# A graph layer on one core: the one-hot gather goes from 8 wide slots a block to 13 slots of two destinations

## The reference, cut to what matters

```python
h = jnp.maximum(_layernorm(x, axis=-1), 0.0)
xs = h[src]
for r in range(4):
    w_r = jnp.where(edge_type == r, edge_weight, 0.0)
    total_msg = total_msg + (xs @ W_rel[r] + b_rel[r]) * w_r[:, None]
agg = segment_sum(total_msg, dst, 625)
agg = agg / jnp.maximum(segment_sum(edge_weight, dst, 625), 1.0)[:, None]
x1 = _layer_norm(h + h @ W_self + b_self + agg, ln1_g, ln1_b)
out = x + _layer_norm(x1 + gelu(x1 @ W_ffn1 + b_ffn1) @ W_ffn2 + b_ffn2, ln2_g, ln2_b)
```

## Time and profile before

| | us |
|---|---|
| median of 3 runs (270.31 to 273.2) | 271.7 |
| the profiled execution, whole | 273.55 |
| its span | 271.4 |

### The profile page before, as it was taken

How to read it: one execution, slowest core, us unless ns; L and a number is a source line. 1 busy time by engine, 2 the same in 40 slices (tenths; PEclk the granted TensorE clock), 3 DMA queues, 4 the chain that set the end, 5 groups by cost and what they waited for, 6 DMA issues and landing times.

```text
span 271.4 us, 3721 instructions
## 1 busy us (share of the span) xinstructions
PE 257.7 (95%) x1443; PEld 212.9 (78%) x1443; DVE 207.1 (76%) x351; ACT 64.1 (24%) x86; POOL 24.6 (9%) x50
## 2 busy tenths in 40 slices
PE   7969999999999999999999998999999999999990
PEld 7857877787887887788887787778888999978770
DVE  2567599698759996899899989995572878955544
ACT  2447111505334014010110220104240663300000
POOL 3193000000000000000010001001020000003211
PEclk9959999999999999999999999999999999999996
DMA  7951232314000510000000000000171075001121
GB/s 188 294 136 65 78 77 80 80 32 127 2 0 1 170 69 1 2 4 0 0 4 3 1 2 4 2 0 3 26 236 51 0 241 146 2 0 38 38 66 47
DMA packets 9453, 15.74 MB, mean 58 GB/s; under 512 B 2413, under 2 KB 2633, under 8 KB 9432
## 3 DMA queue, kind: packets, MB, share of 16 engines
q1 hardware_dynamic: 9168, 15.13, 19.1%
q10 hardware_dynamic: 264, 0.33, 0.6%
HBM read 14.03 MB, written 1.28 MB: 56 GB/s over the span
## 4 chain that ended last, share of the span: by engine, by line
PE 72%; DVE 17%; issue 3%; DMA 3%; DVEq 2%; SPq 1%; ACT 1%; POOL 0%; POOLq 0%; ACTq 0%
PE ps L997 70%; DVE wp L706 4%; DVE keq L701 3%; DMA x<-in_x 3%; DVE eqp L695 3%; DVEq L583 2%; DVE AT_lo L749 1%; SPq L337 1%; DVE wring L580 1%; DVE slot L683 1%; DVE x L761 1%; PE ps L1145 1%; PE ps L1074 1%; PE ps L1004 1%; ACT AT_hi L489 1%
## 5 line engine op out<-in xcount | busy, mean ns | idle before, releaser
L997 PE MATMUL ps<-wring,hT 128*125 128x512 f32 x300 | 75.6, 407 | 2.9 <-DVE hT L601 2.3
L997 PEld LDWEIGHTS ps<-wring,hT 128*125 128x125 f32 x300 | 55.9, 191 | 17.7 <-issue 2.5
L997 PEld LDWEIGHTS ps<-keq,wp 125*128 125x128 f16 x400 | 35.7, 100 | 11.1 <-issue 7.9
L997 PE MATMUL ps<-keq,wp 125*128 125x240 f16 (+5 forms) x400 | 41.9, 261 | 1.7 <-DVE wp L706 1.6
L997 PE MATMUL ps<-T_hi,AT_hi 125*125 125x512 f32 x100 | 40.3, 403 | 0.0
L997 PE MATMUL ps<-T_lo,AT_hi 125*125 125x512 f32 x100 | 39.5, 395 | 0.0
L701 DVE TENSOR_TENSOR keq<-iota_win,slot 125x2240 f16<-125x2240 f16 x25 | 32.9, 1318 | 0.0
L706 DVE TENSOR_TENSOR wp<-eqp,slot 125x1024 f16<-125x1024 f16 x50 | 32.1, 683 | 0.0
L489 ACT CAST AT_hi<-ps 128x1500 fp32r<-128x1500 f32 (+1 forms) x10 | 12.4, 1237 | 64.2 <-PE ps L997 64.2
L997 PE MATMUL ps<-T_hi,AT_lo 125*125 125x512 f32 x100 | 25.9, 404 | 0.0
L997 PEld LDWEIGHTS ps<-T_lo,AT_hi 125*125 125x125 f32 x100 | 18.6, 186 | 4.2
(11 more groups left out here) (130 smaller groups left out, 305.3 us busy)
## 6 DMA issues: line engine op xcount, KB each, us to landing
stage<-in_L_gnn_W_rel SPq DMA_DIRECT2D x8, 512.0 KB, 3.6
stage<-in_L_gnn_W_ffn SPq DMA_DIRECT2D x8, 512.0 KB, 4.0
x<-in_x SPq DMA_DIRECT2D x5, 224.0 KB
x_again<-in_x SPq DMA_DIRECT2D x5, 224.0 KB
out<-ybuf SPq DMA_DIRECT2D x5, 224.0 KB
stage<-in_L_gnn_W_self SPq DMA_DIRECT2D x2, 512.0 KB, 7.6
g_bc<-in_L_gnn_ln_g SPq DMA_DIRECT2D x2, 256.0 KB, 8.4
b_bc<-in_L_gnn_ln_b SPq DMA_DIRECT2D x2, 256.0 KB, 8.3
```

The lines of the kernel that those rows point to most:

```text
L997: return nc.tensor.matmul(o, l, r, start=start, stop=stop, skip_group_check=True)
```

## The change

Each block gets 13 **slots** of two destinations (the last of one), 325 in all. For each slot 128 consecutive edges are chosen on the chip. The edge data lie in 125 partitions of 165 edges, each followed by the first 95 of the next partition (`EW = 260`). VectorE compares each slot's first destination with the destination at every 33rd edge (`ahead`, 6 operations), and the difference of neighbouring comparisons is a 0/1 matrix `chosen`, with a single 1 for each slot over 125 partitions x 5 offsets. TensorE multiplies the edge fields in 16 bits (source and type in one number, destination, weight high, weight low) by it: 25 products in place of the 15 transposes. VectorE makes the keys from the results, doubled in pairs (`pairs`). A block is then read from `pairs` at a fixed place: no register loads and no `slot` copy. The weights are multiplied into the key side, which is now the small one (`kw`, 2 x 13 x 40), `eqp` (13 x 128) is the stationary side, and TensorE makes 26 products of 40 columns a block (the last two of 20). Also changed: the count compares the number of edges found with the number there are, the edge loads are 8 transfers in place of 4 (four on SyncE's queue, ahead of two weight loads, four on ScalarE's), the bias loads 12 in place of 15, and the order of relation and source tile in A is swapped.

```diff
@@ VectorE, start @@
             low_part(0)
-            link(v.tensor_scalar(TF[:, 1, :], raw[:, 0, :], 0.5 - EK / 2, 1.0 / EK, ALU.add, ALU.mult))
+            dve.wait_ge(iotas, 1)
+            for j in range(EG + 1):
+                i = v.tensor_scalar(ahead[0:TN, j, :], slot_d[0:TN, :], edge_d[:, j:j + 1], None, ALU.is_gt)
+            link(i)
             hT_low(0)
...
             hT_low(1)
-            link(v.tensor_scalar(TF[:, 1, :], TF[:, 1, :], TO_INTEGER, -TO_INTEGER, ALU.add, ALU.add))
...
+            v.tensor_tensor(chosen[0:TN, :, :], ahead[0:TN, 0:EG, :], ahead[0:TN, 1:EG + 1, :],
+                            ALU.subtract).then_inc(choice, 1)
...
             low_part(1)
-            dve.wait_ge(first_in, 1)
-            r = firsts(0)
...
-            dve.wait_ge(eT, 1)
-            for f0, f1 in ((0, 3), (3, 5)):
-                i = v.tensor_copy(
-                    fields[0:EK, f0:f1, 0:ET].rearrange("e f (p g) -> e f g p", g=EG),
-                    FIELDS[f0 // 3].rearrange("e (f g p) -> e f g p", f=f1 - f0, g=EG))
-                i.then_inc(turned, 1)
+            dve.wait_ge(picked, 1)
+            link(v.tensor_scalar(Qt[0:EK, :], F_ps, ROW0 - (TN - 1) / 2, 1.0 / TN, ALU.add, ALU.mult))
+            link(v.tensor_scalar(Qt[0:EK, :], Qt[0:EK, :], TO_INTEGER, -TO_INTEGER, ALU.add, ALU.add))
+            link(v.tensor_tensor(drt[0:EK, :], D_ps, slot_d[0:EK, :], ALU.subtract))
+            v.scalar_tensor_tensor(out=pairs[0:EK, 0, :, :], in0=by_two(Qt[0:EK, :]), scalar=float(-TN),
+                                   in1=by_two(F_ps), op0=ALU.mult, op1=ALU.add)
...
@@ VectorE, a block @@
-                v.tensor_tensor(slot[0:EK, :, :, :],
...
-                v.tensor_tensor(by_pairs(keq[0:EK, b % RING, :, :, :].rearrange("e s q d -> e s (q d)")),
-                                by_pairs(iota_win[0:EK, :, :, :].rearrange("e s q d -> e s (q d)")),
-                                spread(1, TR * WD // 2), ALU.is_equal)
...
-                    i = v.tensor_tensor(by_pairs(wp[0:EK, b % RING, part, :, :]), by_pairs(eqp[0:EK, :, :]),
-                                        spread(2 + part, P // 2), ALU.mult)
+                v.tensor_tensor(keq[0:EK, :, :, :], iota_q[0:EK, :, :].unsqueeze(1).broadcast_to([EK, SL, TR, SW]),
+                                pairs[0:EK, 1, at, :].unsqueeze(2).broadcast_to([EK, SL, TR, SW]),
+                                ALU.is_equal).then_inc(key_in, 1)
+                dve.wait_ge(key_in, b + 1)
                 for part in range(2):
+                    i = v.tensor_tensor(kw[0:EK, z, part, :, :, :], keq[0:EK, :, :, :],
+                                        pairs[0:EK, 2 + part, at, :].unsqueeze(2).broadcast_to([EK, SL, TR, SW]),
+                                        ALU.mult)
                 i.then_inc(blk_in, 1)
@@ TensorE, a block @@
-                        last = mm(o[:, :, lo:hi], wp[0:EK, b % RING, part, j, :], keys, j == 0 and part == 0,
-                                  j == SL - 1 and part == 1)
+                        last = mm(o[:, :, lo:hi], eqp[0:EK, b % RING, j, :], kw[0:EK, b % RING, part, j, :, 0:hi - lo],
+                                  j == 0 and part == 0, j == SL - 1 and part == 1)
@@ TensorE, in place of the transposes @@
+            def pick(o, f, s0, s1):
+                for g in range(EG):
+                    i = mm(o, DF[0:TN, f, ES * g:ES * g + EK], chosen[0:TN, g, s0:s1], g == 0, g == EG - 1)
+                return i
...
+            pick(F_ps, 0, 0, NS)
+            pick(D_ps, 1, 0, NS)
+            pe.wait_ge(w_low_in, 1)
+            pick(WH_ps, 2, 0, NS)
+            pick(WL_ps[0], 3, 0, LH)
+            pick(WL_ps[1], 3, LH, NS).then_inc(picked, 1)
```

More of the change, by code:

```diff
@@ L35, in gnn_layer @@
     ROWS_IN = 16 * len(SPANS)
-    EK = TN
-    ET = E // EK
-    EG = 3
-    EP = ET // EG
+    EC = E // TN
+    ES = 33
+    EG = EC // ES
+    EK = P
+    EW = ES * (EG - 1) + EK
+    assert EC * TN == E and EG * ES == EC
     BW = 25
@@ L46, in gnn_layer @@
     NB = NT * HB
-    SL = 8
+    SW = 2
+    SL = -(-BW // SW)
+    NS = NB * SL
+    SLOT_COLS = [(SW * j, min(BW, SW * (j + 1))) for j in range(SL)]
     GROUPS = [[0, 1, 2], [3, 4]]
@@ L92, in gnn_layer @@
     b1_bc = sb("b1_bc", [P, D], F32, 166)
-    wp = sb("wp", [P, RING, 2, SL, P], F16, 168)
-    keq = sb("keq", [P, RING, SL, TR, WD], F16, 176)
-    iota_win = sb("iota_win", [P, SL, TR, WD], F16, 184.75)
-    eqp = sb("eqp", [P, SL, P], F16, 189.25)
-    fields = sb("fields", [P, 5, ET + SL], F32, 191.25)
-    slot = sb("slot", [P, 4, SL, 2], F16, 194.75)
+    eqp = sb("eqp", [P, RING, SL, P], F16, 168)
+    kw = sb("kw", [P, RING, 2, SL, TR, SW], F16, 174.5)
+    keq = sb("keq", [P, SL, TR, SW], F16, 178.75)
+    pairs = sb("pairs", [P, NF, NS, 2], F16, 180)
+    gfields = sb("gfields", [P, 5, EC], F32, 185.25)
+    iota_gen = sb("iota_gen", [P, TR, BW], F16, 188.5)
+    iota_q = sb("iota_q", [P, TR, SW], F16, 189.5)
+    gkeys = sb("gkeys", [P, TR, BW], F16, 189.75)
+    ghot = sb("ghot", [P, P], F16, 190.75)
+    gw = sb("gw", [P, 2, P], F16, 191)
     brel = sb("brel", [P, D], F32R, 200)
@@ L358, in _ @@
                 load_x(c)
+            sp.wait_ge(tails, 1)
+            for f, vec in ((0, src), (2, etype)):
+                flat = vec.rearrange("(p e) -> p e", p=TN)
+                sp.dma_start(raw[0:TN, f, 0:EC], flat).then_inc(src_in, 16)
+                sp.dma_start(raw[0:TN - 1, f, EC:EW], flat[1:TN, 0:EW - EC]).then_inc(src_in, 16)
             load(1)
@@ L367, in _ @@
             for row in SUM_ROWS:
-                for t in range(NT):
-                    sp.dma_start(brel_raw[row + t * R:row + (t + 1) * R, :], b_rel).then_inc(brel_in, 16)
+                for r in range(R):
+                    sp.dma_start(brel_raw[row + r * NT:row + (r + 1) * NT, :],
+                                 b_rel[r:r + 1, :].broadcast_to([NT, D])).then_inc(brel_in, 16)
             for u in range(STAGES, U_REL):
@@ new lines, in _ @@
+            link(v.tensor_scalar(drt[0:EK, :], drt[0:EK, :], -1.0, float(SW), ALU.max, ALU.min))
+            v.scalar_tensor_tensor(out=pairs[0:EK, 1, :, :], in0=by_two(Qt[0:EK, :]), scalar=float(K_STEP),
+                                   in1=by_two(drt[0:EK, :]), op0=ALU.mult, op1=ALU.add)
+            for half, s0, s1 in ((0, 0, LH), (1, LH, NS)):
+                i = v.tensor_copy(pairs[0:EK, 3, s0:s1, :],
+                                  WL_ps[half].unsqueeze(2).broadcast_to([EK, s1 - s0, 2]))
@@ new lines, in _, with build @@
+            i.then_inc(keyed, 1)
+            def build(b):
+                at, z = slice(SL * b, SL * (b + 1)), b % RING
+                if b >= RING:
+                    block_used(dve, b - RING)
+                v.tensor_tensor(eqp[0:EK, z, :, 0:OW].rearrange("e s (n z) -> e s n z", z=2),
+                                iota_p[0:EK, 0:OW].rearrange("e (n z) -> e n z", z=2).unsqueeze(1)
+                                .broadcast_to([EK, SL, OW // 2, 2]),
+                                pairs[0:EK, 0, at, :].unsqueeze(2).broadcast_to([EK, SL, OW // 2, 2]),
+                                ALU.is_equal).then_inc(eq_in, 1)
@@ L803, in _ @@
             self_add(1)
-            dve.wait_ge(iotas, 1)
-            dve.wait_ge(turned, 2)
-            build(0, r[0])
+            dve.wait_ge(iotas, 2)
+            dve.wait_ge(w_pairs, 1)
+            dve.wait_ge(keyed, 1)
+            build(0)
             for c in range(2, NT):
@@ L833, in _ @@
+            build(1)
             dve.wait_ge(vcnt, 1)
-            v.tensor_copy(f_i32[:, NB:NB + 1], COUNT).then_inc(regs_in, 1)
+            link(v.tensor_scalar(vdiff, COUNT[:, 0:1], -1.0, float(E), ALU.mult, ALU.add))
+            v.scalar_tensor_tensor(out=f_i32[:, 0:1], in0=vdiff, scalar=0.0, in1=COUNT[:, 1:2], op0=ALU.max,
+                                   op1=ALU.add).then_inc(regs_in, 1)
             low_part(4)
@@ L851, in block @@
                     if not general_path:
-                        build(b, first[0][i])
+                        build(b)
                     elif i in LAST:
```

332 lines of the change are left out of this document (136 added, 196 removed).

## The result

| | before | with the change |
|---|---|---|
| median of 4 runs, us | 272.45 (270.31 to 273.57) | 256.48 (255.95 to 256.68) |
| profiled execution, us | 273.55 | 256.68 |
| its span, us | 271.4 | 254.9 |

The ratio is 0.9419 with a 95% interval of 0.9354 to 0.9484: 16 us faster, where 259 us and a range of 253 to 268 were forecast. The spans differ by 16.5 us, where the sum had 12.9. The profiled execution of the kernel before is a slow one of its kernel (mean granted clock 0.979, where 31 executions of it beside the experiments had 0.984 to 0.997 and spans of 267.4 to 270.6 us), so a part of the 16.5 us may be that execution's; the medians differ by 16.0 us here and by 15.2 us in experiment 11.

What follows compares the result with a forecast made beforehand. It took TensorE's queue to bound the middle, VectorE close behind, and the start as a third bound. +4.0 - 14.8 - 2.1 = -12.9 us from 273.55 gives 260.65; less 1.85 for that execution, 258.8, in round 259 us, range 253 to 268.

Steps and rivals of the forecast that it cites:

- Blocks on TensorE: 25 blocks in TensorE's queue: 26 pairs of 35 ns each, 0.91 us in place of 1.50, -14.8 us (-20 to -10.3).
- Blocks on VectorE: VectorE's block build: 2.1 us in place of 3.3, 30 us over all blocks, worth only the end of TensorE's waits.
- the waits for `wp`: Three places where TensorE waited for VectorE's weighted tile: they go, -2.1 us.
- The start: Everything before block 0: six operations ahead of `hT_low(0)`, choosing products, keys and waits for self additions, +4.0 us (+2 to +8).
- the low end of the sum: Whole kernel, best case: -20 + 2.5 - 2.1 = -19.6 us, giving 252 us.
- Block 2 behind the branch: Sign against TensorE being fed too slowly: block 2, directly behind a branch, lasts 1.68 us like block 3.
- TensorE cannot be fed so fast: Every block: 26 small pairs in a row meet a floor near 75 ns, 1.95 us a block, 284.9 us; chance 0.13.
- the estimate from the 62 ns a product: TensorE's blocks: at the skill's 62 ns a product a block is 1.61 us and the time 276 us.
- the clock falls at the new wait: TensorE's waits between 38 and 44 us: 7 us at half clock would cost 3.5, 262.3 us; chance 0.15.
- pairs at 50 to 55 ns: TensorE's blocks: 1.35 us each, so they only pay for the start, 270 us; chance 0.06.
- the general path taken: If a slot's edges did not fit its 128, 25 x 165 steps would run, far over 500 us; chance 0.01.

Runs made afterwards that it cites:

- experiment 11: The changed kernel itself again, in six executions, against the kernel before on the same chip: 256.02 us to 271.26, ratio 0.9450.
- Experiments 1 and 2: Changed kernel with every block product issued twice (first), 274.65 us; changed kernel without the 13 products of the weights' low halves a block (second), 246.78 us.
- experiment 3: Changed kernel with each 40-column product split into two of 20 columns, 50 pairs a block: 271.48 us, ratio 1.0024 to the kernel before.
- experiments 4 and 5: Changed kernel with one unread VectorE comparison more a block, 262.78 us; changed kernel without the branch, weights multiplied into the source side again, 262.98 us.
- the six profiles above: Profiles of kernels with the change's own order up to block 0; in them block 0 began between 46.91 and 48.58 us.
- Experiment 7: Changed kernel with `low_part(2)` and two self additions moved ahead of VectorE's key operations: 253.51 us, ratio 0.9359 to the kernel before.
- Experiments 6 and 8: Changed kernel without branch and general path, 254.94 us; Experiment 7 with the fast path directly behind the branch and the general path kept, 252.20 us.
- experiment 9: Changed kernel with the edge weights' maximum behind the row statistics and TensorE's product on it behind eight transposes: 255.02 us, ratio 0.9369.

## Why the prediction was right, and where it was off

The sign, the places and the range were right, and two errors partly cancelled: the blocks gave 4.6 us more than forecast and the branch took back 1.4. By the steps of the prediction:

- **Blocks on TensorE: the mis-sized term.** The forecast was 35 ns a pair and -14.8 us; it is 28 ns and -19.4, close to the low end (27 ns, -20). The step that failed is the choice of the value: I took it near the 33 ns between two weight loads at the start of a block. But those were the first two after a wait, not loads in a running row, and the recorded ends, 0.10 and 0.13 us, give 30 ns to the nearest 10, not 33. The other estimate in the same paragraph, half of an 80-column pair of 40 ns or a little above, is what 40 columns cost. Experiments 1 and 2 give 28 ns from the whole time, for more pairs and for fewer; experiment 3 shows 25 ns at half the columns.
- **Blocks on VectorE.** `eqp` was forecast near 1.0 us and the others near 0.43; recorded are 1004, 422 and 426 ns. From 104 to 185 us TensorE waits for nothing, so the waits for `wp` are gone, -2.1 us. What the text did not say, and experiments 4 and 5 showed, is that without VectorE's saving 6 to 8 of the 16 us would not have come.
- **The start.** Forecast +4.0, measured +3.9, and that it is so close is luck: by the six profiles above it would be +3.1 to +4.7. Six small operations took 1.37 us (forecast 1.2). The first product came 1.9 us later (forecast 0.8): `hT_low(0)` followed the start of these operations by 1.40 us in place of 0.37, and they themselves began 0.87 later, behind a `wmax` that waited for its transfer. At the choosing 0.9 us were left (31.09 for 30.17; forecast 0.4). The choosing took 33.88 - 31.09 = 2.79 us (2.97), the keys 4.1 us (4.5), and the wait for the self addition was 1.94 us recorded, 2.1 between starts (2.3), with another 0.4 among the 30 products behind it (0.6). Experiment 7 gave 2.2 of these 3.9 us back. The columns of the choosing were priced at 0.42 to 0.46 ns; the 80-column steps of 35 and 40 ns give 0.44 and 0.50, so the 0.42 has no row behind it, though the 2.79 us measured are 0.43 a column. And the low end of the sum has +2.5 for the start where the text has +2, which moves it by 0.5 us.
- **The branch: a missed term, +1.4 us.** Block 2 behind the branch lasted as long as block 3, and I used this as a sign that TensorE is not starved of instructions there. That was the wrong place to look: the stops stand ahead of the block and eight products behind it, and block 2 of the changed kernel lasts as long as its others too. I did not ask what ten more pairs a block do there. Experiments 6 and 8 take the stops away, by removing the branch or by turning it.
- **Rival "TensorE cannot be fed so fast".** It fell: 26 and 52 pairs run at 28 ns. With it fell the estimate from the 62 ns a product that the Trainium skill (TensorE: Matmul & The Clock Gate, section "Wait — 56ns, not 53.3ns?") gives for decoding in software. In a weak form it exists, 25 ns at 20 columns, and as the stops behind the branch.
- **Rival "the clock falls at the new wait".** It did not happen in the two profiles of the changed kernel, nor in those of experiments 1 to 6, where TensorE waited 1.93 or 1.94 us at this place and the granted clock stayed at 1.00 from 38 to 48 us; in the change the 30 products behind the wait took 7.63 us. It did happen in that of experiment 9 after a wait of the same length: the granted clock was 0.50 (1.2 GHz) from 39.6 to 43.0 us and the same 30 products took 8.78 us. One of nine such waits: the chance of 0.15 was fair, and the price was 1.15 us rather than 3.5, since the stretch was 3.4 us and the 0.4 us of waiting among these products went with it. What decides between the two is open. Not forecast was a lower mean granted clock of the changed kernel: 0.973 to 0.980 in its ten executions, 0.984 to 0.997 in the 31 of the kernel before beside the experiments. Where in those executions the difference stands is not on record.
- **The other two rivals** (pairs at 50 to 55 ns; the general path taken) show in no row: pairs are 28 ns apart, and the profile has the fast path's 650 products of a block's form, 25 blocks of 26.

## What to carry to other kernels

Price a row of small products with a fresh 16-bit weight load each by the spacing of starts inside a running row, here 28 ns at 40 columns and 25 at 20, not by recorded durations or by the first two behind a wait: between 40 and 20 columns, splitting work into more pairs costs each pair nearly in full. When the bounding engine gets faster, the saving on the engine beside it is a condition and has to be costed as such, by what TensorE would wait without it. Put work that needs nothing new ahead of an engine's wait (2.2 us here), and the likely path directly behind a branch (0.6 to 1.5 us here). And before two profiles are compared instruction by instruction, look at where their granted clock was at half.

## What the runs showed of the hardware that was not expected

- A load of 128 columns in 16 bits and a product of 20 columns together take 25.4 ns (50 in a row), of 40 columns 27.5 ns (52 in a row), while the load is recorded as 97 ns and the product as 190.
- Behind a branch to a path that lies far off, TensorE stopped 0.41 us ahead of a block of small pairs and 1.05 us eight products behind it. The same path placed first had no such stop, with the branch still there.
- Two executions of the same kernel had a granted clock of 0.50 for 6.8 and for 10.2 us at the start, so that first products at 17.77 and 16.88 us led to block 0 at 47.73 and 47.76. In experiment 11 three executions with a mean clock of 0.973 to 0.975 had spans of 254.8 to 255.1 us, and three with 0.979 to 0.980 had 253.2 to 253.7.
- Nearly the same wait, 1.93 to 1.94 us, left the granted clock at 1.00 in eight profiles and was followed by 3.4 us at 0.50 in a ninth.
